# A masked-attention layer re-timed on a clock of groups: clips first, spread broadcasts, 32-column numerator tiles, two residual buffers

## What is computed

```
h = relu(layernorm(x))                       # 8 x 2048 x 256
q, k, v = h @ Wq.T + bq, h @ Wk.T + bk, h @ Wv.T + bv      # 4 heads of 64
scores = clip(q @ k.T / 8, -10, 10);  scores = where(adj == 0, -10, scores)
attn = softmax(scores);  ctx = attn @ v
out = ctx @ Wo.T + bo + h
x = x + layernorm(out) * gamma + beta
```

## Time and profile before

| what | value |
|---|---|
| median of 3 runs | 4936.84 us (4935.59 to 12564.7) |
| the profiled execution's own time | 4939.3 us |
| its span, first to last instruction | 4937.4 us |
| mean granted TensorE clock | 0.98 |
| first clip of the first batch, from the start | 74.79 us |
| end of the last POOL item of the first layer | about 3260.5 us |

### The profile page before, as it was taken

The page is one execution under the profiler, slowest core; times in us unless marked ns, Lnnn a source line. Parts: engine busy times, 40 slices in busy tenths (PEclk is TensorE's granted clock), DMA queues, the critical chain, the costliest instruction groups (busy, mean ns, idle before and its releaser), DMA issues. The chain is left out here.

```text
span 4937.4 us, 78171 instructions
## 1 busy us (share of the span) xinstructions
PE 4623.5 (94%) x31752; PEld 2710.8 (55%) x31752; DVE 3676.7 (74%) x5431; ACT 2913.0 (59%) x3370; POOL 1974.0 (40%) x1415
## 2 busy tenths in 40 slices
PE   7999999998998999999999899948999999999998
PEld 3334334333433433433333343328999999999998
DVE  4776676677578577667667757748889889898896
ACT  3553554555455355355455545518878888888785
POOL 3232233223232223223222323225657667666585
PEclk9999999999999999999999999969999999999999
DMA  5000000000000100000000000011212112111111
GB/s 188 9 9 9 26 18 9 26 9 18 26 9 9 35 9 9 9 26 18 9 26 9 18 9 9 9 42 43 65 41 70 46 53 76 34 65 60 41 57 44
DMA packets 126952, 160.50 MB, mean 33 GB/s; under 512 B 8832, under 2 KB 109184, under 8 KB 126592
## 3 DMA queue, kind: packets, MB, share of 16 engines
q1 hardware_dynamic: 126592, 155.49, 9.9%
HBM read 121.64 MB, written 33.83 MB: 31 GB/s over the span
## 5 line engine op out<-in xcount | busy, mean ns | idle before, releaser
L443 ACT ACTIVATE e_sb<-e_sb 128x1024 f32<-128x1024 f32 x1024 | 1080.4, 1056 | 1189.5 <-DVE e_sb L535 1174.2
L535 DVE SCALAR_TENSOR_TENSOR e_sb<-psS,mask 128x1024 f32<-128x1024 f32 x1024 | 1225.5, 1216 | 466.0 <-PE psS L650 459.2
L1251 PE MATMUL psA<-xy,ring_p 128*128 128x195 bf16 x8192 | 1404.3, 249 | 13.2 <-DVE red L1131 13.2
L1251 PE MATMUL psA<-xy,ring_s 128*128 128x195 bf16 x8192 | 1403.7, 249 | 0.0
L650 PE MATMUL psS<-qT,kT 64*128 64x512 f32 x4096 | 1087.7, 616 | 41.6 <-DVE e_sb L535 41.6
L1051 ACT ACTIVATE ring_s<-eiB,ejb 128x1024 int8<-128x1024 f32 x1024 | 1088.5, 1135 | 9.6 <-PE psA L1251 9.6
L663 PE MATMUL psN<-e_sb,v_sb 128*64 128x512 f32 x4096 | 1002.4, 611 | 0.0
L374 POOL TENSOR_TENSOR ctxT<-ctxT,num 128x512 f32<-128x512 f32 x384 | 486.5, 1276 | 1009.0 <-DVE num L513 1009.0
L1251 PEld LDWEIGHTS psA<-xy,ring_p 128*128 128x128 fp8e4 x8192 | 801.9, 98 | 19.2 <-DVE red L1131 16.4
L1251 PEld LDWEIGHTS psA<-xy,ring_s 128*128 128x128 fp8e4 x8192 | 800.6, 98 | 8.6 <-issue 0.3
L650 PEld LDWEIGHTS psS<-qT,kT 64*128 64x128 f32 x4096 | 460.0, 187 | 448.0 <-issue 233.2
(11 more groups left out here) (106 smaller groups left out, 4020.4 us busy)
## 6 DMA issues: line engine op xcount, KB each, us to landing
eiB<-ei_between SPq DMA_DIRECT2D x64, 512.0 KB, 4.2
xin<-x SPq DMA_DIRECT2D x32, 512.0 KB, 6.8
xr<-x SPq DMA_DIRECT2D x32, 512.0 KB, 3.8
x_between<-hy SPq DMA_DIRECT2D x32, 512.0 KB, 2.9
xin<-x_between SPq DMA_DIRECT2D x32, 512.0 KB, 5.6
xo<-x_between SPq DMA_DIRECT2D x32, 512.0 KB, 4.4
out<-o_sb SPq DMA_DIRECT2D x32, 512.0 KB, 5.3
xr<-adjT SPq DMA_DIRECT2D x12, 512.0 KB, 4.8
```

Source lines behind the costliest of these rows:

```text
L443: act.activation(e_sb[:, s % ES], e_sb[:, s % ES], ACT.Exp, scale=SCALE).then_inc(exp_done, 1)
L535: dve.scalar_tensor_tensor(out=e_sb[:, s % ES], in0=psS[:, s % 2], scalar=-CLIP_RAW, in1=mask[:, kb, cols][:, None, :].to_broadcast([P, 2, ...
L1251: ins = pe.matmul(psA[:, i % BANKS, br * PARTS * XW:(br + 1) * PARTS * XW], part[:, n % RING, k, tt * TW + j * P:tt * TW + (j + 1) * P], x ...
```

## The change

The loops run over groups instead of steps. In each group every engine handles its work in one order: broadcasts and normalizes marked 0, the two steps' scores or clips, broadcasts and normalizes marked 1, then numerators, denominators and projection (PE) or reciprocals, output norm and next norm (DVE). PICKS gives the group and the mark of the 8 broadcasts of a half: offsets 5 to 10 instead of four successive groups. The output projection, the output norm, the residual and the next batch's layernorm get their own group numbers; the next batch's statistics are taken in tiles 0 and 1 and its root once for all 16 blocks. The numerators are four matmuls of 32 columns. e_sb has 8 buffers instead of 6, num 13 instead of 11, xr and hy two instead of one, and beta is added to the residual ahead of time.

```diff
-ES = 6
-NS = GPH + 3
-LN = 13
-SUMS_AT, INV_AT, SPLIT_AT, PICK_AT, RES_AT = 2, 2, 6, 8, 8
-PROJ_AT, LN_AT = 2, 6
-EARLY = 2
-TAIL = HALF + LN_AT + 7 - EARLY
+ES = 8
+NS = 13
+K_AT = (1, 5, 9, 13)
+GAP, GAPG = 18, 9
+MASK_AT = 15
 STATS_AT = (-32, -25, -18, -11)
 H_AT = (-27, -20, -13, -6)
-K_AT = (1, 5, 9, 13)
-MASK_AT = 15
-GAP = 18
+READ_AT, INV_AT, SPLIT_AT = 2, (2, 2, 3, 3), 4
+PICKS = ((5, 1), (6, 0), (6, 1), (7, 1), (8, 0), (8, 1), (9, 1), (10, 1))
+RES_AT, HB_AT = 1, 4
+OUT_AT, STAT2_AT, AGGR2_AT, RSQRT2_AT = 11, 12, 14, (15, 15, 16, 17)
+YN_AT, AFFINE_AT = 20, 28
+TAILG = GROUPS + AFFINE_AT + 2
+XSTATS_AT, RSQRT_AT, TURN_AT = (6, 8, 22, 24), (54, 55, 56, 57), (58, 59, 60, 61)
...
-        xr = sb("xr", [P, TB, F])
-        hy = sb("hy", [P, TB, F])
+        xr = sb("xr", [P, 2, TB, F])
+        hy = sb("hy", [P, 2, TB, F])
...
+        def alive(b, k):
+            return [(b, k)] + ([(b - 1, k + GROUPS + GAPG)] if b and k + GROUPS + GAPG < TAILG else [])
+        def groups_of(b):
...
 
             def load_residual(b, t):
-                if b == 0 and t == 0:
+                n = b * T + t
+                if n >= 2:
+                    sp.wait_ge(o_done, n - 1)
+                else:
                     sp.wait_ge(strip_done, (T - 1) * STRIPS)
...
+            def affine(b, k):
+                t = tile_at(k, HB_AT)
+                if t is not None:
+                    n = b * T + t
+                    pool.wait_ge(hr_done, n + 1)
+                    pool.tensor_tensor(hy[:, n % 2], hy[:, n % 2], b_o[:, None, :].to_broadcast([P, TB, F]),
                                        ALU.add).then_inc(hb_done, 1)
...
-                                       ALU.add).then_inc(o_done, 1)
+                t = tile_at(k, HB_AT + 1)
+                if t is not None:
+                    n = b * T + t
...
+                for k in groups_of(b):
+                    if 2 <= k < GROUPS + 2:
+                        copy_numerators(b, k - 2)
...
+                    if k < GROUPS:
+                        for s in (2 * k, 2 * k + 1):
+                            n = b * BSTEPS + s
+                            act.wait_ge(clip_done, n + 1)
+                            act.activation(e_sb[:, n % ES], e_sb[:, n % ES], ACT.Exp, scale=SCALE).then_inc(exp_done, 1)
                     if b + 1 < nb:
-                        prepare(b + 1, s - BSTEPS)
+                        if k in TURN_AT:
+                            turn_h(b + 1, TURN_AT.index(k))
+                        for v in (2 * (k - GROUPS), 2 * (k - GROUPS) + 1):
+                            prepare(b + 1, v)
...
+            def next_norms(b, k):
+                for t in range(T):
+                    if k in (XSTATS_AT[t], XSTATS_AT[t] + 1):
+                        i = k - XSTATS_AT[t]
+                        if i == 0:
+                            dve.wait_ge(x_in[t], 16 * (b + 1))
+                        for j in (2 * i, 2 * i + 1):
+                            ins = dve.bn_stats(stats[:, j, :], xin[:, t, j, :])
+                        link(ins)
+                        if i:
+                            for j in range(TB):
+                                ins = dve.bn_aggr(mv[:, TB * t + j, :], stats[:, j, :])
+                            link(ins)
+                if k in RSQRT_AT:
+                    part = RSQRT_AT.index(k)
+                    ln_rsqrt(dve, link, part, rs[:, b % 2, :], tmp[:, :], var[:, :], mv)
+                    if part == 3:
+                        scale_means(b, slice(0, BLK))
...
+                for k in groups_of(b):
+                    for bb, kk in alive(b, k):
+                        take_output(bb, kk)
+                        for half, i in picked(kk, 0):
+                            normalize(bb, half * GPH + i)
+                    if k < GROUPS:
+                        clip(b, 2 * k)
+                        clip(b, 2 * k + 1)
+                    for bb, kk in alive(b, k):
+                        for half, i in picked(kk, 1):
+                            normalize(bb, half * GPH + i)
+                        invert(bb, kk)
+                        norm_output(bb, kk)
                     if b + 1 < nb:
-                        prepare(b + 1, s - BSTEPS)
...
+            def numerators(b, g):
+                for u in (2 * g, 2 * g + 1):
+                    (kb, pair), n = place(u), b * BSTEPS + u
+                    pe.wait_ge(exp_done, n + 1)
+                    if u % KPC == 0 and g >= PAIRS:
+                        pe.wait_ge(numcopy_done, b * GROUPS + g - 1)
+                    for part in range(4):
+                        i, col = part // 2, (2 * pair) * D + 32 * part
+                        ins = pe.matmul(psN[32 * part:32 * part + 32, pair, :], v_sb[:, kb, col:col + 32],
+                                        e_sb[:, n % ES, i, :], start=u % KPC == 0, stop=u % KPC == KPC - 1,
+                                        skip_group_check=True)
+                ins.then_inc(num_done, 1)
...
+            def denominators(b, ch):
+                c, n = ch % CPH, b * (GROUPS // PAIRS) + ch
+                if c == 0 and n >= CPH:
+                    pe.wait_ge(sums_read, n // CPH)
+                for kb in range(KPC):
+                    for hd in range(H):
+                        ins = pe.matmul(psD[32 * hd:32 * hd + 32, :], hot[:, c, :],
+                                        e_sb[:, (SPC * n + KPC * (hd // 2) + kb) % ES, hd % 2, :],
+                                        start=c == 0 and kb == 0, stop=c == CPH - 1 and kb == KPC - 1,
+                                        skip_group_check=True)
                 ins.then_inc(sums_done, 1)
...
+            def broadcast(b, half, i):
+                h = b * HALVES + half
+                if i == 0:
+                    pe.wait_ge(r_done, h + 1)
+                if i == 0 and h >= 2 and h % 2 == 0:
+                    pe.wait_ge(y_done, h)
+                elif h or i:
+                    pe.wait_ge(norm_done, h * GPH + i)
+                rows = slice(64 * (i % PAIRS), 64 * (i % PAIRS) + 64)
+                pe.matmul(psM[:, :], pick[rows, i, :], r_s[rows, :], start=True, stop=True).then_inc(bcast_done, 1)
...
+                for k in groups_of(b):
+                    if k == GROUPS and b + 1 < nb:
+                        turn(b + 1, 0, False)
+                    for bb, kk in alive(b, k):
+                        for half, i in picked(kk, 0):
+                            broadcast(bb, half, i)
+                    if k < GROUPS:
+                        scores(b, 2 * k)
+                        scores(b, 2 * k + 1)
+                    for bb, kk in alive(b, k):
+                        for half, i in picked(kk, 1):
+                            broadcast(bb, half, i)
+                    if 1 <= k <= GROUPS:
+                        numerators(b, k - 1)
+                    if k % 2 == 0 and 2 <= k <= GROUPS:
+                        denominators(b, (k - 2) // 2)
+                    for bb, kk in alive(b, k):
+                        project(bb, kk)
                     if b + 1 < nb:
-                        prepare(b + 1, s - BSTEPS, False)
+                        for v in (2 * (k - GROUPS), 2 * (k - GROUPS) + 1):
+                            prepare(b + 1, v, False)
 
```

485 lines of the change are left out of this document (226 added, 259 removed).

## The result

| | before | after |
|---|---|---|
| median of the runs | 4937.84 us (4935.59, 4936.84, 4938.84 and 12564.7) | 4822.07 us (4819.66 to 4822.82, 4 runs) |
| ratio, 95% interval | | 0.9766 [0.9747, 0.9785] |
| profiled execution: its time, its span | 4939.3, 4937.4 us | 4819.66, 4817.9 us |
| mean granted TensorE clock | 0.980 | 0.984 |
| first clip to the last group's clip | 3139.3 us | 3014.6 us |

The account below looks back on a forecast made before the run. PE bounds the layer, with DVE's order costing about 26 us a batch. Savings of 17.8 us a batch times 7, -8 in the last batch and -2.4 in the tail made 135 us, so 4800 us; range 4755 to 4885.

Parts of the forecast that it names:

- Faster by over 2%: Sign for the whole kernel: time below the line at 4838 us, chance 0.66; within 2% 0.28, slower 0.06.
- 32-column numerators: PE's numerators and denominators: one tile shape takes 3.57 us instead of 3.72, 0.15 saved per chunk, 38 us in all.
- The rival in which four tiles run two by two: PE's numerators take 3.7 us instead of 1.87, 957 us more, about 5750 us; chance 0.06.
- the estimate by a cost for each matmul: PE's numerators: about 60 cycles per matmul, 4096 more records add 102 us, ending at 4900; told within a 0.25 rival.
- A lone broadcast: One broadcast behind a group's scores on PE costs 0.33 us, bounds 0.21 to 0.42.
- The wait after a short group: PE's broadcast following a group without denominators waits for DVE 0.15 us twice instead of 0.46 once; group lasts 4.25.
- Spreading thus saves no PE time by itself: Broadcasts over more groups: 0.84 us more PE work per half, 54 us in all (23 to 77).
- Clips first: DVE's order: nothing stands between a group's clips, so late second scores (1.04 us before) go.
- Root held by POOL: Output norm's root in group 15 is held by POOL's addition; PE's second broadcast waits 0.65 us once a tile.
- Tile 3: Last tile of a middle batch: 83.0 us instead of 98.4, as DVE items leave and the clock stays up.
- The gap: Stretch after a batch's four tiles: 56.5 us becomes 59.3, including 4.0 of waits (bounds 0 to 8).
- Tail: After the last group's clip: one POOL item of 2.34 us leaves, so -2.4 us.

Follow-up runs that it names:

- e2_packed: The changed kernel with the eight broadcasts of a half in four successive groups again (offsets 5 to 8); 4845.61 us, ratio 0.9813.
- e6_norms_late: The changed kernel with the whole next norm (statistics, root, turn on ACT) in tile 3 again; 4843.90 us, ratio 0.9812.

## Why the prediction was right or wrong

Faster by over 2% was right, and so were the main terms: the shape of the tiles, the clips first and tile 3. The gain was 116 us instead of 137. By the sum the span would have been 4802.0; it is 4817.9. Of the 15.9 us, 8.3 lie between first clip and last group's clip (124.7 less than before, 133 forecast), 7.2 in the tail (+4.8 where -2.4 was), 1.7 in the second layer and -1.4 ahead of the first clip. The last batch came out right (-7.8, -8 forecast). A batch without the lower clock takes 384.2 us, exactly the forecast. So close a match is luck: by the terms below, errors of some us a batch stand on both sides of it.

- **32-column numerators: right.** 0.15 a chunk (3.58 to the next scores, 3.57 forecast), shown by two experiments. The rival in which four tiles run two by two is out, and so is the estimate by a cost for each matmul: 4096 more records cost nothing.
- **A lone broadcast: mis-sized.** 0.22, the bottom of my bounds, not 0.33. With 32 a batch that is 3.5 us that I charged in excess, 28 in all. Of the 0.42 between its start and that of the numerators, 0.20 are there without a broadcast too; I had taken 0.09.
- **The wait after a short group: mis-sized.** 0.29 with the drain (4.28 against 3.99) and not 0.15, so 2.2 us a batch the other way. The group's length of 4.25 came out right, by two errors that cancel.
- **"Spreading thus saves no PE time by itself": wrong.** I had 0.84 us of work more per half and 0.16 of waits less. By e2_packed it is 0.4 more of work (3.0 a batch, as the price of 0.22 gives) and 0.8 less of waits, net of those in the gap: packed, PE also waits at a second short group and, with 0.93, behind the projection. So the part gains 24 us, where by my sum it loses about 40.
- **Clips first: right**, and with 42 us (6.5 a batch like for like) the largest part. The sum had no term of its own for it; it was in the list of group times.
- **Root held by POOL: right in kind.** Group 15 is 5.55 where 4.51 stands without the root; 1.0 instead of 0.65. The broadcast that waits (1082.63) is the second of a pair after a short group; whether that makes the difference was not tested.
- **Tile 3: right.** 83.9 against 83.0 forecast and 98.4 before. That the next statistics left it is a part of this: e6_norms_late, which puts them back, waits 2.3 us more there. But the lower clock did not leave the kernel: it fell at the gap's first pair of broadcasts, where 0.85 of wait was forecast and 1.45 came. Five times 1.7 us are 8.5, the whole excess between first and last clip; no term and no bound of the sum had it.
- **The gap: right in size (58.8 against 59.3), by parts that differ.** Two pairs waited 0.78 each, v 1.17 instead of 1.4, and 1.7 of the 58.8 are the lower clock. The wait of 1.45 is not in it: the border at 1166.40 lies behind it, so it is in tile 3's 83.9. With the border ahead of that pair (1164.51) tile 3 takes 82.0 and the gap 60.7.
- **Tail: wrong in sign.** I followed only the POOL item that left and not what the new due times carry past the last clip: 7 us. That this work is the cause is argued from the rows.
- **Not forecast:** the second layer takes 1.7 us more. Its code is the same in all versions, and over their traces it takes 1673.8 to 1679.2 us, and the time ahead of the first clip 73.4 to 76.1; so 1.7 us say nothing here.
- **A slip in the range:** 0.21 instead of 0.33 for a lone broadcast is worth 31 us and not 23; 23 is what the whole part costs at 0.21. The low end should have been some 4743, and the result does not hang on it.

## What to carry to other kernels

When a producer has to be waited for, look at which of two unequal groups stands in front of the wait: moving pairs of broadcasts from behind short groups to behind long ones gave 72 us with no item added or removed, more than half of what the whole change gave. Parts undone one at a time may add up to the whole by accident: look for lower clock in each version in windows of a few us, compare batches of the same kind, and expect improvements that take the same waits to overlap. Where work is given later due times, follow what is left past the last iteration, item by item.
